# Scores of the second block from split queries and keys in heads 4 to 13, and the last two output tiles' products apart

## What is computed

```python
# x: (4, 256, 256); H, HK, D, W = 16, 4, 128, 128; two blocks of 128 tokens per batch
q = apply_rope(jnp.dot(x, q_kernel).reshape(b, t, H, D), sin, cos)
k = apply_rope(jnp.dot(x, k_kernel).reshape(b, t, HK, D), sin, cos)
v = jnp.dot(x, v_kernel).reshape(b, t, HK, D)
# a block of queries sees its own block of keys and the one before it
scores = jnp.einsum('bnqhd,bnkhd->bnhqk', qb, kw) * scale
probs = jax.nn.softmax(jnp.where(mask, scores, -1e30), axis=-1)
out = jnp.dot(jnp.einsum('bnhqk,bnkhd->bnqhd', probs, vw).reshape(b, t, H * D), out_kernel)
x = layernorm(x + out)
x = layernorm(x + cross_attention(x, ctx))      # softmax over the context's keys
x = layernorm(x + mixture_of_experts(x))        # 2 shared, 16 routed experts, best 4 per token
```

## Time and profile before

| | before |
|---|---|
| median of 3 runs | 398.79 us (398.7 to 399.05) |
| profiled execution, its own time | 399.91 us |
| its span, first to last instruction | 398.1 us |
| mean granted TensorE clock | 0.998 of 2.4 GHz |
| PE busy | 382.1 us, 96% |
| DVE, ACT, POOL busy | 281.4, 266.1, 190.4 us |
| one window of the attention loop (rows 2 below) | 56.63 us |

### The profile page before, as it was taken

How to read it: one execution, slowest core, us unless ns; L and a number is a source line. 1 busy time by engine, 2 the same in 40 slices (tenths; PEclk the granted TensorE clock), 3 DMA queues, 4 the chain that set the end, 5 groups by cost and what they waited for, 6 DMA issues and landing times.

```text
span 398.1 us, 8200 instructions
## 1 busy us (share of the span) xinstructions
PE 382.1 (96%) x2526; PEld 341.9 (86%) x2526; DVE 281.4 (71%) x778; ACT 266.1 (67%) x661; POOL 190.4 (48%) x326
## 2 busy tenths in 40 slices
PE   8879989999999999999999999999999999999995
PEld 3768879999899999889988878889989998999994
DVE  2978998786878868778767957666658445644455
ACT  3888987785777867687867695665775643534442
POOL 1387456562866653786635665686956200000000
PEclk9999999999999999999999999999999999999999
DMA  8612501000000000000000295232222212343211
GB/s 277 235 38 71 186 0 29 3 0 2 1 3 26 0 0 0 0 0 0 0 0 0 76 370 212 72 103 91 76 92 83 83 54 83 104 139 101 95 58 53
DMA packets 16421, 28.04 MB, mean 70 GB/s; under 512 B 2166, under 2 KB 7784, under 8 KB 16392
## 3 DMA queue, kind: packets, MB, share of 16 engines
q1 hardware_dynamic: 16392, 27.69, 20.7%
HBM read 26.57 MB, written 1.11 MB: 70 GB/s over the span
## 4 chain that ended last, share of the span: by engine, by line
PE 73%; ACT 8%; DVE 7%; issue 6%; POOL 5%; POOLq 0%; DVEq 0%; ACTq 0%
PE bank L635 20%; PE bank L637 19%; PE bank L636 19%; PE bank L761 4%; PE bank L770 3%; PE bank L760 2%; PE bank L733 2%; ACT probs L1007 1%; POOL factor L1541 1%; PE bank L826 1%; ACT xln L1016 1%; ACT probs L1005 1%; ACT swapped L999 1%; DVE by_cos L1258 1%; PE bank L727 1%
## 5 line engine op out<-in xcount | busy, mean ns | idle before, releaser
L935 ACT ACTIVATE hid<-bank,small_sb 128x512 f32<-128x512 f32 x48 | 32.9, 686 | 55.6 <-PE bank L637 47.0
L1156 DVE TENSOR_TENSOR hid<-hid,gate_rows 128x512 f32<-128x512 f32 (+1 forms) x44 | 31.8, 724 | 47.9 <-ACT hid L935 47.7
L636 PE MATMUL bank<-w_lo,hid_hi 128*128 128x256 f32 (+1 forms) x200 | 56.3, 282 | 0.0
L1499 POOL TENSOR_SCALAR nprobs<-probs,rsums 128x128 f32<-128x128 f32 x64 | 25.2, 394 | 56.5 <-DVE rsums L1275 40.9
L1491 POOL TENSOR_TENSOR queryT<-by_cos,by_sin 128x512 f32<-128x512 f32 x32 | 42.5, 1329 | 19.1 <-DVE by_sin L1259 18.3
L1139 DVE TENSOR_TENSOR hid_lo<-hid,hid_hi 128x512 fp32r<-128x512 f32 x48 | 36.2, 753 | 5.4 <-ACT hid_hi L956 5.4
L636 PEld LDWEIGHTS bank<-w_lo,hid_hi 128*128 128x128 f32 (+1 forms) x200 | 37.7, 188 | 2.1
L637 PE MATMUL bank<-x2T_hi,w_lo 128*128 128x512 f32 (+1 forms) x100 | 39.4, 394 | 0.0
L635 PE MATMUL bank<-xT_hi,wq_hi 128*128 128x256 f32 x128 | 37.9, 296 | 1.6 <-DVE by_cos L1258 0.6
L1139 DVE TENSOR_TENSOR pT_lo<-bank,pT_hi 128x384 fp32r<-128x384 f32 x64 | 35.0, 548 | 5.6 <-ACT pT_hi L1022 5.6
L761 PE MATMUL bank<-keyT,queryT 128*128 128x256 f32 x128 | 38.2, 380 | 0.0
(11 more groups left out here) (160 smaller groups left out, 1237.2 us busy)
## 6 DMA issues: line engine op xcount, KB each, us to landing
stage<-in_pieces SPq DMA_DIRECT2D x10, 512.0 KB, 5.1
w_raw<-in_w SPq DMA_DIRECT2D x4, 1024.0 KB, 12.0
gate_rows<-gates_d SPq DMA_DIRECT2D x16, 256.0 KB, 3.1
gate_rows<-gates_d SPq DMA_DIRECT2D x8, 224.0 KB, 3.0
w_raw<-in_w SPq DMA_DIRECT2D x2, 768.0 KB, 7.6
gate_rows<-gates_d SPq DMA_DIRECT2D x8, 192.0 KB, 2.7
gate_rows<-gates_d SPq DMA_DIRECT2D x8, 160.0 KB, 2.5
xraw<-in_xt SPq DMA_DIRECT2D x4, 256.0 KB, 2.9
```

The source lines that it names most:

```text
L636: nc.tensor.matmul(o, sh, ml, start=False, stop=False, **kw)
L935: nc.scalar.activation(hid[:, u % 2, :], z_bank[u % 3][:], ACT.Relu, bias=b1_cols[:, i % NC:i % NC + 1]).then_inc(relu_done, 1)
L1156: nc.vector.tensor_tensor(own, own, gate_rows[rows, i % 3, :], ALU.mult).then_inc(gated, 1)
L1499: nc.gpsimd.tensor_scalar(nprobs[:, u, 0:W], probs[:, u, 0:W], rsums[:, u, 0:1], 1.0, ALU.mult, ALU.mult)
```

## The change

Five edits.

1. In windows 1 to 3, for heads 4 to 13, the second block's product (128 queries by 256 keys) is made of three products of split operands. ACT writes the high parts (`high`: `q_hi` for a slot's two heads' second blocks, 128x256; of k0 one head's keys, 128x256; of k1 two heads', 128x512), POOL writes the low parts (`low_parts`). The keys' parts live in `x2T_hi` and `x2T_lo`, in the columns of the last two batches, so the trace names them so. Seven of each per window: k0, q2, q3, k1, q4, q5, q6. The product waits for the semaphore `low_done`.
2. To make room, `by_sin` is no buffer of its own: the sines are multiplied in place in `swapped`, and ACT's copy therefore waits for POOL's addition of two slots earlier (`rope_add`) instead of the product.
3. In the table, q4 moves from place 4.75 to 4 and q5 from 7.25 to 5.25, in all four windows.
4. At the end, tiles 6 and 7 are groups of their own: the last three steps' products go for tiles 4 and 5 as before, then all for tile 6, then all for tile 7. Tile 6 is now scaled by ACT and stored by a transfer that ACT issues, tile 7 is normalised by DVE and stored by SP.
5. The addition of epsilon before the final square root is done by the square root's own bias.

```diff
-           "k1": 2.75, "q4": 4.75, "v1": 5.5, "v0": 6.5, "q5": 7.25, "q6": 7.75, "q7": 11,
+           "k1": 2.75, "q4": 4, "v1": 5.5, "v0": 6.5, "q5": 5.25, "q6": 7.75, "q7": 11,
+FROM = 4
+HALVED_AT = {"k0": 1.6, "q2": 1.9, "q3": 3.9, "k1": 4.9, "q4": 5.85, "q5": 6.9, "q6": 9.6}
...
-NORM_TILES = ((0, 4), (4, 6), (6, 8))
+NORM_TILES = ((0, 4), (4, 6), (6, 7), (7, 8))
...
+        q_lo = sb("q_lo", [P, 4, 2, W], F32R)
...
-        by_sin = sb("by_sin", [P, 2, HALF], F32, att)
+        q_hi = sb("q_hi", [P, 4, 2, W], F32R, att)
+        by_sin = swapped
...
+        k_hi, k_lo = ([t[:, :, b * T:(b + 1) * T] for b in (B - 2, B - 1)] for t in (x2T_hi, x2T_lo))
...
-                nc.tensor.matmul(o[:, W:3 * W], q[:, W:2 * W], keyT[:, h // G, :],
-                                 start=True, stop=True).then_inc(scored, 1)
+                if not FROM <= h < H - 2 or isinstance(b, int) and b == 0:
+                    mm = nc.tensor.matmul(o[:, W:3 * W], q[:, W:2 * W], keyT[:, h // G, :], start=True, stop=True)
+                else:
+                    e.wait_ge(low_done, halved_count(b, needed))
+                    mm = three(o[:, W:3 * W], q_hi[:, s % 4, h % 2, :], q_lo[:, s % 4, h % 2, :],
+                               k_hi[h // 8][:, h // G % 2, :], k_lo[h // 8][:, h // G % 2, :], True, True)
+                mm.then_inc(scored, 1)
...
-            for u, i in itertools.product((0, 1), range(NI - 3, NI)):
+            for tiles, i in itertools.product(((0, 1), (2,), (3,)), range(NI - 3, NI)):
                 e.wait_ge(hid_done, i + 1)
-                down_pair(i, u)
+                down_tiles(i, tiles)
...
-                        e.wait_ge(rope_mul, rope_count(b, s) - 2)
+                        e.wait_ge(rope_add, rope_count(b, s) - 2)
...
+            def high(b, s):
+
+                if isinstance(b, int) and b == 0:
+                    return
+                j = int(s[1])
+                e.wait_ge(rope_add, rope_count(b, s))
+                if s[0] == "k":
+                    e.wait_ge(w_lo, len(PIECES))
+                    g = 1 - j
+                    ins = nc.scalar.copy(k_hi[j][:, g:, :], keyT[:, 2 * j + g:2 * j + 2, :])
+                else:
+                    ins = nc.scalar.copy(q_hi[:, j % 4, :, :], second_queries(j))
+                ins.then_inc(high_done, 1)
...
-                final_step(nc.vector.tensor_scalar(ln_var[:, a:o], ln_mv[:, a:o, 1:2].rearrange("p t a -> p (t a)"),
-                                                   EPS, None, ALU.add))
...
+            def low_parts(b, s):
+
+                if isinstance(b, int) and b == 0:
+                    return
+                j = int(s[1])
+                e.wait_ge(high_done, halved_count(b, s))
+                if s[0] == "k":
+                    g = 1 - j
+                    ins = nc.gpsimd.tensor_tensor(k_lo[j][:, g:, :], keyT[:, 2 * j + g:2 * j + 2, :],
+                                                  k_hi[j][:, g:, :].bitcast(F32), ALU.subtract)
+                else:
+                    ins = nc.gpsimd.tensor_tensor(q_lo[:, j % 4, :, :], second_queries(j), q_hi[:, j % 4, :, :].bitcast(F32), ALU.subtract)
+                ins.then_inc(low_done, 1)
```

More of the change, by code:

```diff
@@ L96 @@
 NROPE = len(ROPES)
+HALVED = [s for s in ROPES if s in HALVED_AT]
 SPLITS = [s for s in SLOTS if s[0] == "v"]
@@ L107 @@
            "out1": 11},
-    "act": {"next x": 11.6, "slot": 0, "exp": 0.74, "probs_hi": 3, "heads_hi0": 7.25, "heads_hi1": 9.25,
+    "act": {"next x": 11.6, "slot": 0, "high": 0, "exp": 0.74, "probs_hi": 3, "heads_hi0": 7.25, "heads_hi1": 9.25,
             "normed 1": 25.2, "normed 2": 28.95},
@@ L111 @@
             "residual": 22.75, "moments 1": 23, "moments 2": 26.75},
-    "pool": {"next x": 11.7, "slot": 0, "normalise": 0.5, "norm 1": 22.75, "norm 2": 26.75, "keep": 28.75},
+    "pool": {"next x": 11.7, "slot": 0, "low": 0.45, "normalise": 0.5, "norm 1": 22.75, "norm 2": 26.75, "keep": 28.75},
 }
@@ L134, in window_order @@
     for work, lag in WORK_AT[engine].items():
-        if work == "slot":
+        if work in ("high", "low"):
+            events += [(at + lag, work, s) for s, at in HALVED_AT.items()]
+        elif work == "slot":
             events += [(SLOT_AT[s] + lag + LATER.get(engine, {}).get(s, 0), work, s) for s in SLOTS if engine != "pool" or s in ROPES]
@@ L279, in final_count @@
         a, z = NORM_TILES[n]
-        count += {"stats": z - a, "var": z - a + 1, "shift": 2}[w]
+        count += {"stats": z - a, "var": z - a, "shift": 2 if n < len(NORM_TILES) - 1 else 1}[w]
         if (w, n) == (work, g):
@@ L339, in decoder_layer @@
         ln_mv = sb("ln_mv", [P, NT, 2])
-        ln_var = sb("ln_var", [P, NT])
+        ln_eps = sb("ln_eps", [P, 1])
         ln_shift = sb("ln_shift", [P, NT])
@@ L705, in down_pair, with down_tiles @@
             def down_pair(i, u):
+                return down_tiles(i, (2 * u, 2 * u + 1))
+            def down_tiles(i, tiles):
                 h, c = half_of(i)
                 n, r = down_rows(c), i % 3
-                for t in (2 * u, 2 * u + 1):
+                for t in tiles:
                     tok = slice(t * P, (t + 1) * P)
@@ L858, in _ @@
             take_turn("pe", 0, (0, "once"), doers)
+            piece_low(e, "o3")
             with e.Fori(1, B) as b:
@@ L963, in final_std, with final_scale @@
                 a, o = NORM_TILES[g]
+                e.wait_ge(eps_set, 1)
                 e.wait_ge(final, final_count("var", g))
-                nc.scalar.activation(ln_std[:, a:o], ln_var[:, a:o], ACT.Sqrt).then_inc(std_done, 1)
-            def final_scale(g):
-                a, o = NORM_TILES[g]
+                nc.scalar.activation(ln_std[:, a:o], ln_mv[:, a:o, 1:2].rearrange("p t a -> p (t a)"), ACT.Sqrt,
+                                     bias=ln_eps[:, 0:1]).then_inc(std_done, 1)
+            def final_scale(g, tiles):
                 e.wait_ge(final, final_count("shift", g))
-                for t in range(a, o):
+                for t in tiles:
                     if t in BY_ACT:
@@ L1067, in _ @@
                 e.sem_inc(s, 1)
-            doers = {"next x": lambda b, _: split_x(b + 1), "slot": slot, "exp": softmax_exp, "probs_hi": probs_hi, "once": once,
+            e.sem_inc(high_done, len(HALVED))
+            doers = {"next x": lambda b, _: split_x(b + 1), "slot": slot, "high": high, "exp": softmax_exp, "probs_hi": probs_hi, "once": once,
                      "heads_hi0": lambda b, g: heads_hi(b, g, 0), "heads_hi1": lambda b, g: heads_hi(b, g, 1),
@@ L1127, in _ @@
                 if i == NC + 8:
-                    final_scale(0)
+                    final_scale(0, range(HT))
             hid_high(NI - 2)
@@ L1563, in _ @@
                 e.sem_inc(s, AHEAD)
-            doers = {"next x": lambda b, _: x_low(b + 1), "once": once, "slot": slot, "normalise": normalise, "keep": keep, "norm 1": lambda b, _: layer_norm(b, 0),
+            e.sem_inc(low_done, len(HALVED))
+            doers = {"next x": lambda b, _: x_low(b + 1), "once": once, "slot": slot, "low": low_parts, "normalise": normalise, "keep": keep, "norm 1": lambda b, _: layer_norm(b, 0),
                      "norm 2": lambda b, _: layer_norm(b, 1)}
```

41 lines of the change are left out of this document (28 added, 13 removed).

## The result

The changed kernel took 405.05 us (median of 4 executions, 403.79 to 406.13), the kernel before 398.75 us beside it (4 executions, 398.37 to 399.05): a ratio of 1.0145, 95% interval 1.0122 to 1.0168. The change makes the kernel 4.4 to 6.3 us slower; 3.4 were forecast. Two of the first comparison's four executions, at 406.1 us, show a lower mean clock (0.995 and 0.996; told of under x11); the other two took 403.8 and 404.0 us. The profiled execution of the changed kernel took 404.02 us, its span is 402.2 us.

What follows compares the result with a forecast made beforehand. PE's own work was taken to bound the attention loop, DVE and ACT window 0. Terms −2.1 + 3.0 + 2.1 + 0.4 + 0.4 − 0.4 = +3.4 us on 398.79 gave 402.2 us, range 398.4 to 405.0.

Steps and rivals of the forecast that it cites:

- A, products: Scores of ten heads in three windows: three split products replace one plain, 0.07 us less per head, 2.1 us less.
- counts in full: Attention loop: PE's own work sets the pace, so every saved product shortens the time by its whole length.
- B, slot n: First layer norm: q5 ahead of out1 makes PE's wait 1.53 us against 0.53, 3.0 us in three windows.
- C, low parts at head 4: Heads 4 and 5 wait for POOL's low parts of k0 and q2: 0.7 us per window, 2.1 in three.
- D, q0: What heads 11 to 13 save, PE waits at q0 for the next x's low part, in two windows: +0.4 us.
- E, window 0: ACT's swapped copy for q2 waits 0.65 us longer for k0's addition: +0.4 us, from −0.3 to +1.1.
- Part of it should be absorbed: Window 0: part of the swapped copy's 0.65 us delay should be absorbed by the waits behind it.
- q4 and q5 come earlier ... with no work added or removed: Window 0: earlier q4 and q5 on all engines, work unchanged, no separate gain or loss counted.
- rival 2: Window 0 gains up to 1.8 us from early q4 and q5, with smaller loop waits: 397.1 us; chance 0.13.
- F, the end: Behind the last product: tile 7's statistics alone, `ln_var` gone, scale on DVE; about 0.4 us earlier (0.3 to 0.5).
- Its signs: At the end: last tensor instruction 2.0 to 2.1 us behind the last product's start, then 2.5 us to the end.
- Added work at nothing: ACT's and POOL's other parts hide under PE at no cost; a failed cover costs 0.6 us in each window.

Runs made afterwards that it cites:

- x11: Changed kernel with group 3's out1 ahead of v0, its residual and moments ahead of v0's low part on DVE: 405.54 us against 398.8, ratio 1.0161.
- x5: The kernel before once more, no edit, one recorded execution: 398.72 us.
- x1: The changed kernel once more, no edit, on another chip (the second comparison): 402.61 us against 398.2, ratio 1.0115.
- x8: Changed kernel with q5 back at 7.25 and unsplit, k0's and q2's parts earlier, sines in their own buffer again: 397.24 us against 399.25, ratio 0.9951.
- x12: x8 with only heads 4 to 7 in split products, parts of k0, q2 and q3 alone: 396.49 us against 398.77, ratio 0.9942.
- x2: Kernel before with only the table's two places changed, q4 at 4 and q5 at 5.25: 400.42 us against 398.2, ratio 1.0059.
- x3: Changed kernel with q5 back at 7.25 and not split, so heads 10 and 11 plain: 400.46 us against 398.2, ratio 1.0073.
- x4: Changed kernel with the parts of k0 and q2 at 0.8 and 1.2 instead of 1.6 and 1.9: 400.22 us against 398.2, ratio 1.0066.
- x9: x8 with all scores plain products, high and low parts still written but read by nothing: 398.22 us against 398.8, ratio 0.9985.
- x10: x8 with q5 at 5.25 and split again, and group 3's out1 ahead of v0: 401.45 us, ratio 1.0066.
- x6: Kernel before with only the sines multiplied in place, the buffer's room kept reserved: 400.74 us against 399.25, ratio 1.0038.
- x7: Kernel before with only the new end (tiles 6 and 7 apart, epsilon in the square root's bias): 398.99 us against 399.25, ratio 0.9992.

## Why the prediction was right, and where it wasn't

The direction was right, and the size nearly: 402.2 us was forecast with a range to 405.0. The second comparison's 402.61 lies near its middle. The first one's 405.05 is 0.05 us beyond its upper end, and got there by something that no term had, the lower clock of two of its four executions; the other two, 403.8 and 404.0, lie inside. By its own steps, with recordings of the same pattern compared (before with after, x5 with x1):

- **A, products, −2.1.** Right in its price: 0.59 for 0.66 us per head. By the four passes that the Trainium skill (FP8 and Floating Point Precision, TensorE Precision Notes) gives for true FP32 it would be 0.55, an estimate; the trace does not show that, the row's 0.07 held. But x8 and x12 show that "counts in full" was wrong for heads 8, 9, 12 and 13, each of which stands ahead of a wait for a chain.
- **B, slot n, +3.0.** Right in mechanism and size: the wait went from 0.38 to 1.50 and from nothing to 1.13, 1.12 to 1.13 per window for 1.0. x2 makes it alone (0.97), x3 undoes it. The step of 0.78 did shrink to 0.20. The 0.64 was to stay; it did not, but another step, beside another sine product, took 0.75 or 0.40 in its place.
- **C, low parts at head 4, +2.1.** Right: 0.8 us per window in x4 for the 0.7 worked out. k0's part took 0.73 (0.74 worked out from the rows), q2's 1.18: 0.45 more, beside k1's sine product, where 0.43 was taken from `nprobs`. The 0.1 us taken for the signal stood in no row; PE started 0.05 us behind the low part's end.
- **D, q0, +0.4.** Not seen: the wait for `xT_lo` is 0.6 us in all, 0.7 before. In x8 it does grow, if little: 0.8 us at the weight loads, of which 0.3 now also show at PE, where before shows none. The two rows are of one and the same wait, so the 1.1 us of x12's expectation counts it twice. In x12 it is back at 0.7. Why the changed kernel itself is spared was not tried.
- **E, window 0, +0.4.** Here a step failed, and the sum hid it. Window 0 is 0.75 to 0.80 us longer (62.35 for 61.60 and 61.55). "Part of it should be absorbed" was wrong: edit 2 costs 1.3 us alone and 1.5 with the places (62.35 for x2's 60.86), since it makes two copies wait and not one. And "q4 and q5 come earlier ... with no work added or removed", at nothing, was wrong too: the places gain 0.7 us, which is the first half of rival 2. That +0.4 comes within 0.4 of the measured +0.8 is luck: two errors of 1.1 and 0.7 us against each other. The steps that failed are these two.
- **F, the end, −0.4.** Right in the sum: 4.46 for 4.94 us. Its signs were not: the last instruction was to start 2.0 to 2.1 us behind the last product with 2.5 us to the end, and it is 1.7 and 2.8. The first sign was at odds with the term itself: by the earlier trace rows it was 395.07 − 393.16 = 1.91 before, and it was to become shorter.
- **Added work at nothing.** Right away from head 4: in x9 POOL is busy 204.3 us, in x5 188.9, and PE has no new wait. For q5's part that holds only behind the long wait at n: in x10, without this wait, it cost 0.6 us in each window.

The sum then reads +0.8 (E) + 3 × 1.3 (the windows: −0.7 + 1.13 + 0.8, and 0.05 to 0.2 that no term has) − 0.5 (F) = 4.2 us, for 4.4 measured beside x1. The term that was left out altogether is the lower clock in window 0. Of 37 executions of the kernels with the sines in place (the changed one, x1, x3, x4, x6, x11) 14 show a mean clock of 0.992 to 0.996 and lie 1.9 to 3.4 us above the shortest of their kernel, two of the four in the first comparison, at 406.1 us. Of 47 executions of the kernels with the sine buffer (x2, x5, x7 to x10, x12) none has such a clock; of 61 of the kernel before beside them one has 0.996 and is 0.5 us above the shortest. So the lower clock goes with edit 2, which also makes the wait for `attT` 2.1 us instead of 1.8. That this wait brings it about, and that it is the same stretch each time, is inferred from x11's recording; none of the other 13 was recorded.

## What to carry to other kernels

Where a product is moved ahead of the start of a long chain, the work that covers the chain shrinks by the product's whole length (1.44 us here, of which 1.1 came back as wait, since the chain itself got some 0.5 shorter and the split products of heads 8 and 9 took away another 0.14); write down chain and cover for each wait before touching the order, since freeing one wait by another order (x11) can put it whole at the next. A saved instruction counts only if no chain that started earlier ends between it and the next common point: here half of the split heads (x12) gave all of the gain that could be measured. And before giving up a buffer, count every user two places behind it, in the phase where the engines, not PE, set the pace.

## What the runs showed of the hardware

- POOL's tiny steps and DVE's product of two SBUF operands hold each other up in one of two ways, from starts that lie 0.02 and 0.03 us apart: POOL's 0.19 us step through and the next at 0.40 (x1), or held at 0.75 beside DVE's 0.68 (after). What decides between them is not shown. The Trainium skill (SBUF — State Buffer, "SBUF: two separate sides") says that the two exclude each other, and that whichever starts first has the port for its whole instruction. The trace agrees on the length, 0.75 being DVE's 0.68 and little more, but not on who is held: it is POOL's step, which has the earlier start (161.24 for 161.26); and in x1 DVE's product took only 0.03 us longer, with POOL's step beside it for 0.16. So a chain on POOL has two lengths, 0.37 us apart here, which made 0.8 us between the loops of two executions of one kernel.
- The granted clock fell to 1.2 GHz for about 3 us in window 0 (0.64, then 0.51 over stretches of 2 us), behind a stretch in which PE was busy 0.67 of 2 us. The kernel before has a similar gap there (PE busy 2.24 of the 4 us from 28 to 32, the changed one 1.89, x11 1.88), and of its 61 executions one shows so low a mean clock. The changed kernel's two recordings have x11's gap and kept the full clock; what exactly decides it stays open.
- A split product of 128x256, weights included, stood 0.12 us behind the one before, and a low part of 128x256 on POOL took 0.73 us, as the halved addition had suggested (0.74).
